# Two stage boundaries of a selective-scan and memory kernel rearranged at once: VectorE's correction and diagonals ahead of the scan, projection beside the memory's setup behind it

## The reference, cut to what matters

```python
# layer 0: a selective-scan (Mamba) block over 2 images of 4096 positions, 512 channels
xn = layernorm(gn(x)) * ln_w + ln_b
xin, z = split(xn @ in_proj_w.T)                 # 1024 channels each
xs = silu(causal_conv4(xin) + conv_b)
dt, B, C = split(xs @ x_proj_w.T)                # 32, 16, 16
delta = softplus(dt @ dt_proj_w.T + dt_proj_b)
h = exp(delta * A) * h + delta * xs * B          # along the positions, 16 states for each channel
y = (h * C).sum(states) + xs * D_skip
x = x + (y * silu(z)) @ out_proj_w.T
# layer 1: a memory of 1024 rows of 512 numbers
score = l2norm(gn(x)) @ l2norm(m).T
idx = argmax(score); counts, esum = segment sums of gn(x) by idx
new_m = m * 0.999 + esum / (counts + 1e-6) * 0.001
x = x + softmax(score) @ new_m
```

## Time and profile before

| | |
|---|---|
| plain runs, median of 3 | 4971.79 us (4964.84 to 4975.98) |
| the profiled execution | 4989.84 us |
| its span (first to last instruction) | 4988.1 us |
| mean granted clock of TensorE | 0.974 of full |
| front's last operation on GpSimd ends | 1194.2 |
| first and last recurrence of the scan | 1227.0, 3829.4 |
| group parameters begin, assignment begins | 3871.1, 3898.2 |

### The profile page before, as it was taken

How to read it: one execution, slowest core, us unless ns; L and a number is a source line. 1 busy time by engine, 2 the same in 40 slices (tenths; PEclk the granted TensorE clock), 3 DMA queues, 4 the chain that set the end, 5 groups by cost and what they waited for, 6 DMA issues and landing times. The chain is left out here.

```text
span 4988.1 us, 120130 instructions
## 1 busy us (share of the span) xinstructions
PE 4655.8 (93%) x47160; PEld 2950.1 (59%) x47160; DVE 4106.8 (82%) x4324; ACT 2984.3 (60%) x6070; POOL 3419.2 (69%) x1712
## 2 busy tenths in 40 slices
PE   4999999993899999999999999999999699999999
PEld 4666666661455555555555555555554588887787
DVE  7888888872999999999999999999997667776332
ACT  2666666664777776767777777777764444554111
POOL 0576777765999999999999999999997222222000
PEclk9999999996999999999999999999999899999999
DMA  5344433433233323332333323332331111112453
GB/s 202 115 152 150 151 142 130 150 141 126 68 97 96 95 82 93 97 93 86 90 100 101 90 83 95 95 95 89 95 96 53 66 76 76 76 76 81 183 200 135
DMA packets 191783, 538.35 MB, mean 108 GB/s; under 512 B 15824, under 2 KB 15840, under 8 KB 181840
## 3 DMA queue, kind: packets, MB, share of 16 engines
q1 hardware_dynamic: 185920, 480.31, 28.8%
q0 software_dynamic: 5104, 51.35, 2.6%
q10 hardware_dynamic: 288, 0.00, 0.0%
HBM read 329.22 MB, written 202.38 MB: 107 GB/s over the span
## 5 line engine op out<-in xcount | busy, mean ns | idle before, releaser
L920 POOL TENSOR_TENSOR sc_hc<-sc_hc,sc_c_rep 128x1024 f32<-128x1024 f32 x1024 | 2397.7, 2369 | 170.0 <-ACT sc_state L941 167.7
L1158 DVE TENSOR_TENSOR_SCAN sc_hc<-sc_da,sc_state,sc_ring 128x512 f32<-128x512 f32 x2048 | 2431.4, 1260 | 51.1 <-PE sc_ring L1065 42.8
L980 ACT ACTIVATE sc_da<-sc_delta,l_neg_a 128x512 f32<-128x512 f32 x2048 | 1351.7, 707 | 0.0
L1065 PEld LDWEIGHTS sc_ring<-sc_diag,sc_dut 64*64 64x64 f32 x32768 | 890.1, 133 | 718.7 <-issue 718.6
L1065 PE MATMUL sc_ring<-sc_diag,sc_dut 64*64 64x128 f32 x32768 | 1102.3, 275 | 24.6 <-DMA sc_w_out<-in_w_out 17.2
L1075 PE MATMUL sc_y_ps<-sc_hc,sc_fold 128*64 128x512 f32 x4096 | 1004.7, 612 | 28.2 <-POOL sc_hc L920 21.7
L941 ACT ACTIVATE sc_state<-sc_hc 128x2 f32<-128x2 f32 x1024 | 206.0, 201 | 647.4 <-DVE sc_hc L1158 647.4
L1085 PE MATMUL sc_o_ps<-sc_yg,sc_w_out 128*128 128x512 f32 x1024 | 556.1, 630 | 2.9 <-ACT sc_o_sb L964 2.1
L1366 POOL TENSOR_TENSOR l_count<-l_count,as_oh 128x1024 f32<-128x1024 f32 x64 | 182.4, 2850 | 505.8 <-DVE as_oh L1549 505.8
L1075 PEld LDWEIGHTS sc_y_ps<-sc_hc,sc_fold 128*64 128x64 f32 x4096 | 251.1, 137 | 415.4 <-issue 379.6
L71 PE MATMUL fr_mm<-fr_xn_hi,l0f_w_in_hi 128*128 128x512 f32 x1024 | 438.4, 428 | 26.3 <-DVE fr_delta L671 11.8
(11 more groups left out here) (166 smaller groups left out, 6572.1 us busy)
## 6 DMA issues: line engine op xcount, KB each, us to landing
sc_duz<-spill SPq DMA_DIRECT2D x128, 768.0 KB, 5.9
sc_delta<-spill SPq DMA_DIRECT2D x256, 256.0 KB, 4.0
spill<-fr_z SPq DMA_DIRECT2D x64, 512.0 KB, 2.8
spill<-fr_u SPq DMA_DIRECT2D x32, 1024.0 KB, 8.7
spill<-fr_du SPq DMA_DIRECT2D x32, 1024.0 KB, 4.3
spill<-fr_delta SPq DMA_DIRECT2D x32, 1024.0 KB, 6.4
sc_c_rep<-bc SPq DMA_DIRECT2D x128, 256.0 KB, 4.4
soft<-as_et SPq DMA_DIRECT2D x16, 2048.0 KB, 6.3
```

What stands on the lines that cost most here:

```text
L920: nc.gpsimd.tensor_tensor(hc[:, p], hc[:, p], c_rep[:, 2 * q:2 * q + 2, :], ALU.mult).then_inc(s_hp, 1)
L980: nc.scalar.activation(da[:, p % 4, r, :], delta[:, i % 2, p % 2, :], ACT.Exp, scale=keep.neg_a[:, c:c + 1]).then_inc(s_da, 1)
L1065: done = nc.tensor.matmul(to[:, :, k::4], dut[rows, i % 2, k, HALF * h:HALF * h + HALF], diag[rows, u, 4 * q + c:4 * q + 4:2, k, :], start ...
L1158: nc.vector.tensor_tensor_scan(hc[:, p, r, :], da[:, p % 4, r, :], ring[:, SLOT[at], r::2], state[:, i, 2 * p + r:2 * p + r + 1], ALU.mult ...
```

## The change

*Front's end (the last chunk only).* GpSimd does nothing for it. VectorE does the correction, each operation on half a tile (128x2048). ScalarE finishes the first half up to Ln before the second half's absolute values. SyncE stores delta and du each when its half is done.

*Scan's start.* The 64 diagonals of chunk 0 become 16 VectorE operations, each four diagonals from two broadcast inputs. c_rep's first quarter is loaded ahead of du/u/z(0,1), b_row(1) ahead of w_out, and TensorE waits for w_out before the first projection, a chunk later.

*Scan's end.* The scan block ends with the last gate. A new block holds the last chunk's projections with their additions, statistics and stores, and `memory_setup`, which is gone as a block of its own; m is loaded at this block's start, iota and v behind the first x1 store. Buffers of the scan that the new block needs or that must not be overwritten share their storage with those of layer 1 (`delta` with `v`, `yg` with `et`, `w_out` with `sums` and so on), in unchanged sizes.

```diff
@@ front, SyncE
-            store_delta(NG - 1, 0)
-            store_delta(NG - 1, 1)
+            for h in range(2):
+                sp.wait_ge(s_dl, KD * (NG - 1) + 4 * h + 4)
+                store(NG - 1, delta, DELTA, h, st_dl)
+                sp.wait_ge(s_du, KD * (NG - 1) + 4 * h + 4 + KD)
+                store(NG - 1, du, DU, h, st_du)
@@ front, GpSimd
             def main(b, j, after, first):
+                if after(1) is None:
+                    return
@@ front, ScalarE
-            for m in range(KD):
-                absolute(NG - 1, m)
             for h in range(2):
+                for m in range(4 * h, 4 * h + 4):
+                    absolute(NG - 1, m)
                 exp(NG - 1, h)
-            for h in range(2):
                 log(NG - 1, h)
@@ front, VectorE
+            def correct_log(g, h):
+                rows = slice(4 * h, 4 * h + 4)
+                n = KD * g + 4 * h + 4
+                dve.wait_ge(s_r, 2 * g + h + 1)
+                dve.wait_ge(s_ln, 2 * g + h + 1)
+                nc.vector.tensor_tensor(du[:, rows, :], du[:, rows, :], r[:], ALU.subtract).then_inc(s_c1, 4)
+                dve.wait_ge(s_c1, n + 4)
+                nc.vector.tensor_tensor(du[:, rows, :], du[:, rows, :], e[:, rows, :], ALU.add).then_inc(s_c2, 4)
+            def give_delta(g, h):
+                rows = slice(4 * h, 4 * h + 4)
+                n = KD * g + 4 * h + 4
+                dve.wait_ge(s_rl, n + KD)
+                dve.wait_ge(s_c2, n + KD)
+                nc.vector.tensor_tensor(delta[:, rows, :], delta[:, rows, :], du[:, rows, :], ALU.add).then_inc(s_dl, 4)
+                dve.wait_ge(s_dl, n)
+                nc.vector.tensor_tensor(du[:, rows, :], u[:, rows, :], delta[:, rows, :], ALU.mult).then_inc(s_du, 4)
...
-            for m in range(KD):
+            for m in range(4):
                 positive(NG - 1, m)
             rounded(NG - 1, 0)
+            correct_log(NG - 1, 0)
+            for m in range(4, KD):
+                positive(NG - 1, m)
+            give_delta(NG - 1, 0)
             rounded(NG - 1, 1)
+            correct_log(NG - 1, 1)
+            give_delta(NG - 1, 1)
@@ scan, SyncE
             delta_in(0, 0)
+            c_in(0, 0)
             duz_in(0, 1)
-            for q in range(4):
+            for q in range(1, 4):
                 c_in(0, q)
-            sp.dma_start(w_out[:], d.w_out).then_inc(s_w, 16)
             sp.wait_ge(s_bt, 1)
             row_in(1)
+            sp.dma_start(w_out[:], d.w_out).then_inc(s_w, 16)
             chunks(sp, body)
@@ scan, ScalarE
-            act.wait_ge(s_fold, 1)
-            for e in range(NDIAG):
-                make_diag(0, 0, e)
@@ scan, TensorE
             turn(0, 0)
-            pe.wait_ge(s_fold, 1)
-            pe.wait_ge(s_w, 16)
@@ scan, VectorE
+            dve.wait_ge(s_fold, 1)
+            dve.wait_ge(s_col, 1)
+            for n in range(NS):
+                nc.vector.tensor_tensor(diag[:, 0, n], fold[:].rearrange("p (k d) -> p k d", k=1).broadcast_to([P, 4, HALF]),
+                                        b_col[:, :, n:n + 1].broadcast_to([P, 4, HALF]), ALU.mult).then_inc(s_diag, 4)
             chunks(dve, body, before)
             gate(NG - 1, 1, KD - 1)
@@ the new block, one engine after the other
+            sp.dma_start(keep.m[:], d.m.rearrange("(k p) c -> p k c", p=P)).then_inc(keep.m_loaded, 16)
+            x1_out(sp, NG - 2, 3)
+            x_in(sp, NB - 1, NJ - 1, 1)
+            sp.dma_start(keep.iota[:], d.iota.broadcast_to([P, KM])).then_inc(keep.iota_loaded, 16)
+            sp.dma_start(keep.v[:], d.x1[0]).then_inc(keep.x_loaded, 16)
+            x1_out(sp, NG - 1, 0)
...
+            keep_projection(act, NG - 2, 3)
+            act.wait_ge(keep.m_loaded, 16)
+            for k in range(KK):
+                if k:
+                    act.wait_ge(s_sq, k)
+                nc.scalar.activation(sq[:], keep.m[:, k, :], ACT.Square, accum_out=norm[:, k:k + 1]).then_inc(s_sq, 1)
+            act.wait_ge(s_sq, KK)
+            nc.scalar.activation(norm[:], norm[:], ACT.Sqrt).then_inc(s_root, 1)
+            for m in range(3):
+                keep_projection(act, NG - 1, m)
+            for n in range(4):
+                high(n)
+            keep_projection(act, NG - 1, 3)
+            for n in range(4, 8):
+                high(n)
...
+            for m in range(3):
+                project(pe, NG - 1, 1, m, 0, KD)
+            pe.wait_ge(s_mn, KK)
+            for n in range(4):
+                turn_m(n)
+            project(pe, NG - 1, 1, 3, 0, KD)
+            for n in range(4, 8):
+                turn_m(n)
...
+            statistics(dve, NB - 1, NJ - 2, KC - 1)
+            dve.wait_ge(s_root, 1)
...
+            for k in range(KK):
+                nc.vector.tensor_scalar(mn[:, k, :], keep.m[:, k, :], norm[:, k:k + 1], None, ALU.mult).then_inc(s_mn, 1)
+            for m in range(3):
+                statistics(dve, NB - 1, NJ - 1, m)
+            for n in range(4):
+                low(n)
+            statistics(dve, NB - 1, NJ - 1, 3)
+            for n in range(4, 8):
+                low(n)
```

More of the change, by code:

```diff
@@ L742, in scan @@
         w = Place(nc, ctx, "sc")
-        c_rep = w.sb("c_rep", [P, NS // 2, T])
-        b_row = w.sb("b_row", [NS, T])
-        b_col = w.sb("b_col", [P, 4, NS])
-        diag = w.sb("diag", [P, 2, NS, 4, HALF])
-        fold = w.sb("fold", [P, HALF])
-        delta = w.sb("delta", [P, 2, 2, T])
-        duz = w.sb("duz", [P, 4, 3, T])
-        dut = w.sb("dut", [P, 2, 4, P])
-        da = w.sb("da", [P, 4, 2, T])
-        hc = w.sb("hc", [P, PAIRS, 2, T])
-        state = w.sb("state", [P, KD, SCANS])
-        yg = w.sb("yg", [P, 2, KD, T])
-        w_out = w.sb("w_out", [P, KD, DIM])
-        x_res = w.sb("x_res", [P, 2, T])
-        o_sb = w.sb("o_sb", [P, 2, T])
-        ring = w.ps("ring", [P, 3, 2 * T])
-        y_ps = w.ps("y_ps", [P, T])
+        delta = keep.v[:].rearrange("p (u h) t -> p u h t", u=2)
+        dut = keep.iota[:].rearrange("p (u k d) -> p u k d", u=2, k=4)
+        da = keep.m[:].rearrange("p (s r) t -> p s r t", r=2)
+        yg = keep.et
+        w_out = keep.sums
+        x_res = keep.e[:, 0, :].rearrange("p (u t) -> p u t", u=2)
+        o_sb = keep.count[:].rearrange("p (u t) -> p u t", u=2)
         o_ps = w.ps("o_ps", [P, T])
@@ L788, in scan @@
         st_x1 = [w.sem(f"x1_stored{i}") for i in range(2)]
-        block = ctx.enter_context(nc.Block())
         x_view = d.x.rearrange("b (k p) (j r) w -> b j p k (r w)", p=P, j=NJ)
@@ L800, in begun, with x_in, x1_out, add_x @@
             return not isinstance(value, int) or value > 0
+        def x_in(sp, b, j, m):
+            g = b * NJ + j
+            sp.wait_ge(st_x1[m % 2], 32 * g + 16 * (m // 2) + 16)
+            sp.dma_start(x_res[:, m % 2, :], x_view[b, j][:, m, :]).then_inc(s_x[m % 2], 16)
+        def x1_out(sp, g, m):
+            sp.wait_ge(s_res, KC * g + m + 1)
+            sp.dma_start(d.x1[g][:, m, :], x_res[:, m % 2, :]).then_inc(st_x1[m % 2], 16)
+        def add_x(pool, g, m):
+            pool.wait_ge(s_x[m % 2], 32 * g + 16 * (m // 2) + 16)
+            pool.wait_ge(s_o, KC * g + m + 1)
+            nc.gpsimd.tensor_tensor(x_res[:, m % 2, :], x_res[:, m % 2, :], o_sb[:, m % 2, :], ALU.add).then_inc(s_sum, 1)
+        def keep_projection(act, g, m):
+            act.wait_ge(s_op, KC * g + m + 1)
+            before = KC * g + m - 1
+            if begun(before):
+                act.wait_ge(s_sum, before)
+            nc.scalar.activation(o_sb[:, m % 2, :], o_ps[:], ACT.Copy).then_inc(s_o, 1)
+        def project(pe, g, u, m, first, last):
+            if isinstance(g, int) and (g, m, first) == (0, 0, 0):
+                pe.wait_ge(s_w, 16)
+            for i in range(first, last):
+                before = KC * g + m
+                if i == 0 and begun(before):
+                    pe.wait_ge(s_o, before)
+                done = nc.tensor.matmul(o_ps[:], w_out[:, i, m * P:(m + 1) * P], yg[:, u, i, :],
+                                        start=(i == 0), stop=(i == KD - 1))
+            if last == KD:
+                done.then_inc(s_op, 1)
+        def statistics(dve, b, j, m):
+            g = b * NJ + j
+            dve.wait_ge(s_sum, KC * g + m + 1)
+            nc.vector.bn_stats(keep.stats[:, b * KC + m, j, :], x_res[:, m % 2, :]).then_inc(s_res, 1)
         def chunks(eng, body, before=None):
@@ L1206, in memory_setup @@
[L1206 to L1208 removed]
+        step = w.sem("norm_step")
+        s_mn = w.sem("m_scaled")
+        s_tr = w.sem("m_transposed")
+        s_hi = w.sem("m_high")
+        s_lo = w.sem("m_low")
         HALVES = [(c, f) for c in range(KC) for f in range(KM // T)]
         PER = T // P
[L1212 to L1223 removed]
@@ L1274, in assign @@
         oh = w.sb("oh", [P, 2, TT, KM], F32R)
-        e = w.sb("e", [P, 2, KM])
+        e = keep.e
         es = w.sb("es", [P, TT])
         er = w.sb("er", [P, TT])
```

(2 more changed lines are left out.)

754 lines of the change are left out of this document (357 added, 397 removed).

## The result

| | before | after |
|---|---|---|
| plain runs, median | 4973.89 us (4964.84 to 4976.31, 4 runs) | 4924.70 us (4920.47 to 4925.77, 4 runs) |
| ratio | | 0.9903, 95% interval [0.9886, 0.992] |
| profiled execution (span) | 4989.84 (4988.1) | 4925.77 (4924.1) |

What follows compares the result with a forecast made beforehand. TensorE, busy 93% of the span, bounds the stages but not the gaps at two boundaries, where the change acts. 30.4 + 15.3 + 9.3 = 55.0 us off 4971.8 gives 4917; range 4904 to 4933.

Steps and rivals of the forecast that it cites:

- Front's end: End of the front: VectorE's correction replaces 32 GpSimd operations, scan begins 30.4 us sooner; bounds 27 and 31.5.
- The marks that the forecast set by the clock: Signs: VectorE's front operations end near 1166, scan's first DMA near 1171, assignment's first operation near 3843.2.
- Rival C: Table loads: ScalarE must empty itself before each, priced at 3.8 us more, time 4921; chance 0.04.
- Scan's start: First recurrence 15.8 us sooner with VectorE's diagonals last; 15.3 after the queue's 0.5, bounds 9 and 16.5.
- one of the things named as making the prediction wrong: Scan's start: the prediction is wrong if the first recurrence waits for anything but the diagonals.
- The queue: SyncE's loads at the scan's start: b_row(1) and delta(0,1) land about in time; 0.5 us taken off for all.
- Rival A: Scan's start held by the DMA: b_row(1) again takes 14.2 us, TensorE 7.3 late; time 4923, chance 0.09.
- Scan's end: Last gate to assignment: m's chain overlaps the projections, TensorE waits between projections 0 and 1; 9.3 us, bounds 2.6 and 12.4.
- Rival B: Scan's end gives nothing: TensorE's wait for ScalarE's squares costs what overlap saves; gain 48, time 4924, chance 0.08.
- D: Rival in the scan: slower pace, 0.43 us more per channel block eats all 55; 4994 at 0.6, chance 0.03.
- E was to move by no more than 5: Sign: the prediction is wrong if the time from first recurrence to last gate (2607) moves by more than 5.

Runs made afterwards that it cites:

- e4: Changed kernel with b_row(1) issued behind c_rep's first quarter instead of all four; 4926.07 us, 0.9887 of the kernel before.
- e6: e4 with w_out's load moved behind du/u/z(0,3), in the first chunk's second channel block; 4925.65 us, 0.9895 of the kernel before.
- e2: Kernel before with only the scan's start changed (VectorE's diagonals, SyncE's order, TensorE's waits); 4966.93 us, 0.9969 of the kernel before.
- e5: The changed kernel once more, nothing altered; 4922.25 us, 0.9893 of the kernel before.
- e7: Changed kernel with ScalarE copying projection 0 out before m's squares; 4922.83 us, 0.9889 of the kernel before.
- e9: The changed kernel again, untouched, in another call; 4930.39 us, 0.9897 of the kernel before.
- e3: Kernel before with only the scan's end changed, with the shared storage; 4969.09 us, 0.9979 of the kernel before.
- e8: Changed kernel plus eight unused 128x128 matmuls on TensorE in each channel block of chunk 0; 4923.78 us, 0.9883 of the kernel before.
- e10: Changed kernel with the edits of e6 and e7 together; 4916.51 us, 0.9868 of the kernel before.
- e11: e10 plus e8's matmuls from the second channel block on; 4907.48, 4909.41 and 4915.42 us in three runs, 0.9862 of the kernel before.
- e1: Kernel before with only the front's end changed; 4944.26 us, 0.9928 of the kernel before.

## Why the prediction was right

**Front's end, 30.4 forecast, 30.5 measured** (66.81 - 36.31). The order of the chain, the table loads and the operations' length are as forecast. VectorE's chain from first to last correction takes 22.4 (1158.18 - 1135.77), the forecast's figure too. That is partly luck: an operation that takes the result of the one before comes at a pitch of 2.40 and not 2.33, but where the next one does not, the pitch is 2.21 (1138.17 to 1140.38). The marks that the forecast set by the clock (1166, 1171, 3843.2) lie 3 to 8 us behind the measured times, as the last chunk's first absolute value stood at 1127.14 and not 1134.93, ahead of every edit. Two small sizes were off and cancel: the first correction comes 8.6 us behind the first absolute value, not 9.2, and from VectorE's end to `fold` go 5.3, not 4.8. Rival C (ScalarE empties before a table load) is refuted here as before: the load starts 0.01 us behind the last absolute value (1127.14 + 2.07, 1129.22).

**Scan's start, 15.8 forecast to the first recurrence, 16.4 measured** (25.28 - 8.84). The 16 diagonals cost 0.34 each, not 0.40, near the lower of the two rows that bounded them. So they were not last: the first recurrence waited 0.24 us for TensorE's fill, which waited for `dut`, and that for the DMA of du/u/z. That was one of the things named as making the prediction wrong, and on this point it was, by 0.24 us. In e4 and e6 the first recurrence waited 0.56 and 0.65 us for TensorE in the same way.

**The queue, 0.5 forecast, 3.3 measured** (C, 29.6 against 26.3; 2.4 to 3.6 in e2, e5, e7 and e9, which have the same order there). This is the mis-sized term, and two loads are in it. The prediction had b_row(1) land 8 us after its issue, behind c_rep's loads, and gave TensorE 1.3 us of slack on top. But in the rows it went by, c_rep's loads land later one after the other, and the 10.0 of the earlier trace rows is the last of them, the one ahead of b_row(1); a load behind it was to be put at 10 or more. It landed after 10.2, and TensorE wanted it from 1178.4 on. The second is delta(0,1), forecast to land 15.8 us behind the first recurrence and to be wanted at 16.8; it landed at 17.6, and in e4, where nothing hides it, ScalarE wanted it from 14.4 on (1192.93 - 1178.53). e4 removed the first wait alone and C stayed (29.0 against e5's 28.7); with both loads early C came back to 26.6. Whether moving w_out alone would have been enough was not run. Rival A had b_row(1) land after 14.2 and TensorE 7.3 late; it was 3.8 late, and not by Rival A's mechanism, for w_out stood behind it.

**Scan's end, 9.3 forecast, 9.8 measured; 8.4 to 10.0 in e3 to e6, e8 and e9.** The wait between projections 0 and 1 is what the order puts there, with m at 8.8 against 8.4 forecast. Projection 1 was put at 9.1 (7.13 + 2.0 for the clock); it took 8.85 here and 8.70 to 10.18 in the other executions that have the wait, and 7.13 in e7, e10 and e11, which have not. What was not foreseen: in some executions projection 0 is slow as well (10.06 here, 8.61 in e5, 10.19 in e7, 8.83 in e9), as the granted clock falls behind the 2.36 us wait of the last `add_up` or, in e9, early in the projection. In the changed kernel this was hidden behind m's squares (TensorE's idle time shrank to 6.03, and projection 1 began 17.3 us behind the last gate, as in e3 and e6, where projection 0 took 7.13), so it cost nothing. TensorE's window in the changed kernel, behind the wait between the projections, with the granted clock third from the end:

```profile
3800.70:3807.30 6.60, 3.40 (x4) 1.51 (x5) 3.84 (x9) 3.09 (x7) 1.45 (x1) 0.50 0.33 137
```

The granted clock is 0.50 there, the lower level, behind 6.03 us of idleness. The Trainium skill (TensorE: Matmul & The Clock Gate, Part 1) says that idleness costs the array its clock, and the trace agrees.

e7 and e10 show what the order of one copy was worth: 7.1 us against e5, 10.4 against e9. Of the 3.3 between the two, 3.1 is projection 0, which was slow in e7 (10.19) and at full speed in e10 (7.13): where the copy goes first, nothing hides a slow projection 0 any more.

**Rival B** (the tail gives nothing) and **D** (the scan loses its pace) fall: F gains 8.4 us or more in every execution with the new block, and from the second chunk on the chunks last 161.7 in before and after alike, but for a few that are longer in both.

**E was to move by no more than 5, and moved by 6.5.** 3.3 is the queue and 1.1 the first chunk (163.5 to 164.6); the rest is spread over later chunks. In e5 and e9, the same program, E is 2604.6 and 2612.2, 3.1 under before and 4.4 over it. The limit was set tighter than executions of one kernel keep.

**The total.** 4924.70 against 4917: 2.1 us because before had 4973.89 in that call and not 4971.79, and 5.8 in the gain, 49.2 against 55.0. The queue explains 2.8 of that, and the three small surpluses (0.1 at the front's end, 0.6 at the scan's start, 0.5 at its end) work the other way. The rest, some 4 us, can't be assigned: the gain in the other two calls was 56.7 and 50.4, so it is within what the medians tell. That the total came within 8 us of the forecast therefore says less than the stages do.

## What to carry to other kernels

Price a boundary between stages by its own chains: three gaps gave 30, 16 and 10 us, and all three could be read from the rows ahead of time to within 0.6; what was missed, 3.3 us, lay behind the second gap and not in it. Where loads are moved in one queue, look at what the engines want in the 20 us behind, and count what is issued ahead of each load: in two orders a load of 32 KB landed 0.2 us behind the one ahead of it, 10.2 and 5.9 us after its issue. A load that is wanted a chunk later belongs behind all that are wanted now. When one late load is mended and the stage does not shorten, look for the next one that it hid. And an engine that serves two chains in a written order should first release the one whose buffer is single: one copy ahead of eight squares was worth 7 us and more.

## What was not expected of the hardware

The scan's first chunk, with the same work for the engines in every kernel but e8 and e11, takes either 156.7 to 158.4 us or 163.5 to 164.6, with the granted clock of its windows of 40 us at 1.00 or at 0.91 to 0.96. One program had both: 164.6 in the first profile after, 156.7 in e5, 164.5 in e9. TensorE is not full there (34 of 40 us), having no projection to do.

The length follows from the number of times that the granted clock falls in the chunk, from 1.00 to 0.50. In five executions it does not fall, or only until 2 us behind the first gate (e1, e3, e4, e5, e8: 156.7 to 156.9). In four it falls once, in the last channel block, behind a wait of TensorE of 1.95 to 2.31 us (e2, e6, e10, e11: 158.2 to 158.4). In before it falls six times (163.5), in after, e7 and e9 seven times (164.5 to 164.6), each time at the wait of 1.56 us for GpSimd in a channel block, and each of these blocks takes 1.1 us more. In the short chunks the same wait goes by without a fall. The matmuls added in e8 and e11 do away with that wait, and neither has a fall there; but of the eleven executions without them seven had none there either, so two are too few to tell. What decides which of the two an execution gets is open. Of the five executions with the changed queue order and nothing else in the chunk's beginning three were long (after, e7, e9), of the other six without added matmuls one (before). That is a hint that the waits behind b_row(1) matter, and no more.

The plain runs seem to bear the same mark. Of the thirteen runs of the changed kernel (after, e5, e9), the four with the lowest mean granted clock, 0.979, took 4925.77 to 4937.23 us, and the nine with 0.980 to 0.982 took 4920.47 to 4926.53. Both profiled executions with the long chunk are among the four.

It is why a profile of one execution can be off by 7 us in a stage that was not touched, and why the stage by stage reading, not the difference of two spans, prices an edit of this size.
